# Cross attention with split operands: both tail products of neighbouring PV steps ahead of their small products

## The reference, cut to what matters

```python
q = split_heads(x @ w_q)                       # 20 heads of 32
k, v = split_heads(text @ w_k), split_heads(text @ w_v)
out_text = softmax(q k^T / sqrt(32)) v
k_ip, v_ip = split_heads(ip @ w_k_ip), split_heads(ip @ w_v_ip)
out_ip = softmax(q k_ip^T / sqrt(32) + mask_ip) v_ip   # mask from the boxes and the query's place
out = merge_heads(out_text + out_ip) @ w_out + b_out + x
```

## Time and profile before

| | us |
|---|---|
| median of 3 runs | 709.34 |
| lowest and highest | 707.80, 711.19 |
| the profiled execution | 710.03 |
| its span, first to last instruction | 708.0 |
| TensorE busy with matmuls in the span | 685.1 (97%) |
| TensorE's weight loads | 633.3 (89%) |
| VectorE busy | 534.3 (75%) |
| ScalarE busy | 291.0 (41%) |
| GpSimd busy | 215.0 (30%) |
| mean granted TensorE clock, share of full | 0.988 |

### The profile page before, as it was taken

The page is one execution under the profiler, slowest core; times in us unless marked ns, Lnnn a source line. Parts: engine busy times, 40 slices in busy tenths (PEclk is TensorE's granted clock), DMA queues, the critical chain, the costliest instruction groups (busy, mean ns, idle before and its releaser), DMA issues.

```text
span 708.0 us, 19244 instructions
## 1 busy us (share of the span) xinstructions
PE 685.1 (97%) x6570; PEld 633.3 (89%) x6570; DVE 534.3 (75%) x1689; ACT 291.0 (41%) x636; POOL 215.0 (30%) x371
## 2 busy tenths in 40 slices
PE   6998999999999999999999999999999999999987
PEld 4787678989899999999998999999999999899876
DVE  3344468797879788887978787878888797978773
ACT  1132353351617262534435161726353442516160
POOL 5312006042423324150504242332415050424233
PEclk9999999999999999999999999999999999999989
DMA  9979616444436262534444353626353444434320
GB/s 297 379 212 213 152 37 142 130 105 111 123 83 163 67 173 77 147 84 140 100 133 103 105 130 77 171 67 168 82 142 90 134 101 121 112 82 118 80 64 37
DMA packets 52512, 89.40 MB, mean 126 GB/s; under 512 B 9440, under 2 KB 23520, under 8 KB 52460
## 3 DMA queue, kind: packets, MB, share of 16 engines
q1 hardware_dynamic: 51024, 86.09, 45.3%
q10 hardware_dynamic: 1068, 1.66, 0.9%
q0 software_dynamic: 384, 1.18, 0.8%
HBM read 39.21 MB, written 10.62 MB: 70 GB/s over the span
## 4 chain that ended last, share of the span: by engine, by line
PE 84%; SPq 5%; DMA 4%; DVE 3%; issue 1%; ACTq 1%; ACT 1%; POOL 0%; DVEq 0%
PE psum L1086 38%; PE psum L1147 9%; PE psum L1193 9%; PE psum L1172 5%; PE psum L1177 5%; SPq L414 4%; PE psum L1016 3%; PE psum L1201 3%; PE psum L1202 2%; PE psum L1216 2%; PE psum L954 2%; PE psum L1046 1%; PE psum L1199 1%; DMA q_stack<-mask_scratch 1%; DMA k_stack<-k_lo 1%
## 5 line engine op out<-in xcount | busy, mean ns | idle before, releaser
L570 POOL TENSOR_TENSOR attn<-o_parts 128x128 f32<-128x128 f32 x160 | 73.0, 457 | 418.3 <-DVE o_parts L901 388.0
L860 DVE TENSOR_REDUCE neg_max<-psum 128x2 f32<-128x292 f32 x320 | 144.6, 452 | 48.8 <-PE psum L1147 48.5
L1086 PE MATMUL psum<-wo_both,at_hi 128*128 128x320 f32 x640 | 153.6, 314 | 0.0
L1147 PE MATMUL psum<-k_stack,q_stack 104*128 104x154 f32 x640 | 113.6, 288 | 5.5 <-DMA q_stack<-mask_scratch 3.5
L1086 PE MATMUL psum<-xt_hi,wq_hi 128*128 128x256 f32 x400 | 114.6, 287 | 1.1 <-DVE q_lo L852 1.1
L1086 PE MATMUL psum<-xt_lo,wq_hi 128*128 128x256 f32 x400 | 111.7, 279 | 0.0
L1086 PE MATMUL psum<-xt_hi,wq_lo 128*128 128x256 f32 x400 | 111.5, 279 | 0.0
L1086 PEld LDWEIGHTS psum<-wo_both,at_hi 128*128 128x128 f32 x640 | 110.1, 189 | 0.0
L888 DVE TENSOR_TENSOR p_lo<-psum,p_hi 128x512 f16<-128x512 f32 x160 | 107.8, 682 | 2.8 <-ACT psum L714 2.7
L712 ACT ACTIVATE p_hi<-psum 128x512 f16<-128x512 f32 x160 | 95.2, 595 | 29.7 <-PE psum L1172 29.5
L1193 PE MATMUL psum<-v_tail,p_tail 128*128 128x264 f32 x320 | 102.4, 401 | 1.8 <-ACT p_tail L716 0.9
(11 more groups left out here) (96 smaller groups left out, 1268.3 us busy)
## 6 DMA issues: line engine op xcount, KB each, us to landing
q_stack<-q_hi SPq DMA_DIRECT2D x128, 96.0 KB
x_in<-in_x SPq DMA_DIRECT2D x16, 640.0 KB, 5.3
x_res<-in_x SPq DMA_DIRECT2D x16, 640.0 KB, 5.5
out<-out_sb SPq DMA_DIRECT2D x32, 320.0 KB
q_stack<-q_hi SPq DMA_DIRECT2D x128, 64.0 KB
q_stack<-q_lo SPq DMA_DIRECT2D x60, 96.0 KB
q_stack<-q_lo SPq DMA_DIRECT2D x60, 64.0 KB
q_stack<-aux_a SPq DMA_DIRECT2D x48, 64.0 KB, 2.4
```

The source lines that it names most:

```text
L570: nc.gpsimd.tensor_tensor(cols, o_parts[:, qt, 0:4, :], o_parts[:, qt, 4:8, :], ALU.add).then_inc(att_half, 1)
L860: nc.vector.tensor_reduce(dst[:, :, 0], src[:, :, 0:TEXT], AX_X, ALU.max, negate=True)
L1086: last = nc.tensor.matmul(ps, l(c), r(c), start=(i == 0), stop=(i == len(terms) - 1))
L1147: last = nc.tensor.matmul(scores[sc % 2][:, i * CTX:(i + 1) * CTX], q_stack[0:ROW_MAX, query_slot(h), P * qt:P * (qt + 1)], k_stack[batch] ...
```

## The change

The constant `TAILS_AHEAD = 2` is new. At a PV step TensorE looks at up to two PV steps in a row from there on. It issues the waits and the tail product of each that has not had its tail yet, and only then the 12 small products of its own step. A step whose tail has been issued already goes straight to its small products. In the run of three this gives tail (1,1), tail (2,0), small (1,1), small (2,0), tail (2,1), small (2,1). In the run of two it gives tail (3,0), tail (3,1), small (3,0), small (3,1). Nothing is added or taken away, and only TensorE's stream is altered.

```diff
+TAILS_AHEAD = 2
...
+            def neighbours(order, at):
+
+                run = []
+                while len(run) < TAILS_AHEAD and at < len(order) and order[at][1] == "PV":
+                    run.append(tuple(order[at][2]))
+                    at += 1
+                return run
...
-                for stage, kind, args, gen, sc in it.steps():
+                order, tails = it.steps(), []
+                for at, (stage, kind, args, gen, sc) in enumerate(order):
...
                     if kind == "PV":
+                        run = neighbours(order, at)
+                        for g, qt in run if at not in tails else ():
+                            if isinstance(t, int) and t == 1 and (g, qt) == (0, 0):
+
+                                pe.wait_ge(s_vc, 5)
+                                pe.wait_ge(s_vsplit, 3 * V_PARTS)
+                            if qt == 0:
+
+                                pe.wait_ge(exp_done, t * ST_ALL - ST_ALL + 1 + max(ST_TURN[(g, u)] for u in range(3)))
+                                pe.wait_ge(p_split, t * 10 - 10 + 2 * g + 2)
+                            ahead = run.index((g, qt))
+                            free_general(it, gen + ahead)
+
+                            nc.tensor.matmul(product_1[it.general_bank(gen + ahead)][:, 0:8, :],
+                                             p_tail[:, -g % P_SLOTS, P * qt:P * (qt + 1)],
+                                             v_tail[batch][:, g, :].rearrange("p (e d) -> p e d", d=VW), start=True, stop=False)
+                            tails.append(at + ahead)
                         g, qt = args
-                        if isinstance(t, int) and t == 1 and (g, qt) == (0, 0):
-
-                            pe.wait_ge(s_vc, 5)
-                            pe.wait_ge(s_vsplit, 3 * V_PARTS)
-                        if qt == 0:
-
-                            pe.wait_ge(exp_done, t * ST_ALL - ST_ALL + 1 + max(ST_TURN[(g, u)] for u in range(3)))
-                            pe.wait_ge(p_split, t * 10 - 10 + 2 * g + 2)
-                        free_general(it, gen)
                         queries = slice(P * qt, P * (qt + 1))
-
-                        nc.tensor.matmul(product_1[it.general_bank(gen)][:, 0:8, :], p_tail[:, -g % P_SLOTS, queries],
-                                         v_tail[batch][:, g, :].rearrange("p (e d) -> p e d", d=VW), start=True, stop=False)
                         for j in range(4):
```

## The result

The changed kernel has a median of 711.55 us in 20 runs, the kernel before 708.81 us in 20. The ratio is 1.0041 with a 95% interval of 1.0024 to 1.0058: 0.4% slower, small but clear of no change. The profiled execution has a span of 710.3 us against 708.0.

A forecast was written before the change was run, and what follows sets the result against it. PE was taken to bound nearly each step; 12 blocks at 0.22 us, three at 0 and 0.2 in the last add 2.8 us to the median of 709.34, giving 712.1 us, range 708.3 to 714.6.

The forecast's parts named there:

- What the change gains: On PE, tails (2,0) and (3,1) behind another tail each save 0.08 us of weight load: 0.16 us a block.
- Rival 2: A tail behind a tail hides no weight load; PE loses 0.08 us more a block, 713.3 us; chance 0.08.
- What it delays: Small products of (1,1) end 0.45 us later, DVE's chain slips, tail (3,1) waits for PV(2,0)'s bank: 0.22 us a block.
- Tail (3,0) reacts 0.07 us after p_lo: PE's load for tail (3,0) starts 0.07 us after DVE ends p_lo of ST(3,1), at 264.48 against 264.47 today.
- Made good in blocks 1, 8 and 15: PE's waits there for query DMAs, 0.48, 0.26 and 0.26 us, cover the 0.22 us delay, so these blocks cost nothing.
- The last block: Tail (4,0) follows p_lo of ST(4,1), which has DVE's delay of 0.20 us: a cost of 0.2 us.
- The sum: Whole kernel: 12 blocks at 0.22 us, 3 at 0, the last 0.2: together 2.8 us, 712.1 us, 0.4% slower.
- Rivals 1 and 3: 1: DVE's slip stays covered, block 38.24 us, 706.8 us, chance 0.14; 3: slip reaches PE whole, 716.1 us, chance 0.06.
- rival 3: DVE still late at PE's score banks, up to 0.45 us a block, block over 38.75 us, 716.1 us; chance 0.06.

The follow-up runs named there:

- pairs_same_group: Changed kernel, but tails paired as (2,0) with (2,1) and (3,0) with (3,1); against the kernel before: ratio 0.9958, in a second comparison 0.9984.
- late_readout: Kernel before, TensorE order untouched; DVE waits for PV(2,0) too before reading out PV(1,1): 714.8 us, ratio 1.0107 to the kernel before.
- three_ahead: Changed kernel, but in the run of three all three tails come before any small products: 718.41 us, ratio 1.0141 to the kernel before.
- low_part_first: Changed kernel, with DVE writing p_lo of ST(3,1) before the readout of PV(1,1): 711.98 us, ratio 1.0050 to the kernel before.
- pair_first: Changed kernel, but only tail (2,0) drawn ahead, behind tail (1,1); (3,0) and (3,1) as before: 709.3 us, ratio 0.9995 to the kernel before.

## Why the prediction was right, point by point

- *What the change gains.* Right. A tail behind a tail starts after 0.22 us, tail (2,1) came 0.08 us sooner. Rival 2 does not hold for these loads. What reaches the end of a block was a little less, on the mean 0.11 and 0.13 us for two pairs in place of 0.16; in pairs_same_group about 0.02 us of it is lost again between the start of ST(4,2) and tail (4,0) (2.33 us in place of 2.30), and in its first profile the second loop gained only 0.08 us. Why is open.
- *What it delays.* Right, to 0.01 us: reciprocal at 1.44 us (1.44 forecast), readout of (2,0) at 3.67, load of tail (3,1) at 3.72, ST(4,2) at 4.96 (4.95), block 38.62 (38.62). That this chain is the cause is shown from four sides: without the slip there is no cost (pairs_same_group), with a slip and no new order there is one (late_readout, where a larger slip comes in at tail (3,0)), a larger slip costs more (three_ahead), a shortened chain on DVE costs less (low_part_first).
- *Tail (3,0) reacts 0.07 us after p_lo.* A size that was off. That figure came from the first block, which is written out singly. In the loops it is 0.12 us (pair_first, late_readout, and the change itself: `p_lo` ends at 265.60, the load starts at 265.73). In the full change it did not move the time, since tail (3,1) waits longer anyway.
- *Made good in blocks 1, 8 and 15.* Wrong for blocks 8 and 15. The DMA waits there did not cover the delay: behind them PE waits for DVE, and DVE was as late as PE. The delay passed through block 8 as through its neighbours (to the next tail (1,1) it grew from 1.80 to 2.03 us, 378.52 - 376.72 and 417.27 - 415.23), and through block 15 at least as far as tail (4,1), 0.22 us. Two blocks at 0.22 us, 0.4 us of the sum, were left out wrongly. For block 1 it is open. Its DMA wait did not shrink (0.48 us before, 0.54 after), and from its tail (1,1) to the next one it took 40.83 us in place of 39.95; but this stretch scatters from 39.95 to 42.51 us over the nine profiles.
- *The last block.* Right: tail (4,0) comes 0.17 us later after tail (1,1) (6.50 in place of 6.33), 0.2 was forecast.
- *The sum.* It came out at 2.8 us forecast and 2.7 us measured (711.55 - 708.81), but partly by chance: with blocks 8 and 15 it would have been 3.3 us (14 x 0.22 + 0.2), and the interval of 1.7 to 4.1 us does not tell the two apart. In the two profiles, the delay is 0.48 us at block 2, grows by 3.01 us to block 15 and ends at 2.3 us. Part of the last stretch ran faster in the profile after, at a granted clock of 0.95 of full speed in place of 0.84 (part of the stretch at the lower level of 1.2 GHz). From the windows of both, before and after:

```profile
670.00:702.00 32.00, 28.12 (x246) 24.50 (x247) 20.80 (x63) 14.16 (x29) 11.98 (x21) 0.84 0.16 43
...
670.00:702.00 32.00, 26.26 (x251) 22.92 (x251) 22.62 (x72) 14.08 (x29) 11.46 (x21) 0.95 0.15 42
```

- *Rivals 1 and 3.* Neither. No block of the change is near 38.24. In the first loop none is above 38.75; in the second, where a block took 38.47 to 38.52 us before, they take 38.70 to 38.77. The longest is past the forecast's mark by 0.02 us, but the price there is 0.22 to 0.30 us and not the 0.45 of rival 3. DVE had again 0.70 us of idle time ahead of Q 4 (0.67 before), so its backlog ended there.

## What to carry to other kernels

A tuned order holds back work for a reason that the busy engine's own profile does not show: each product drawn forward delays the signal of those behind it. Before moving one, look for who starts within 0.05 us of that signal, follow its list in order, and ask which later wait its last item feeds. Here the remedy was to choose the pair whose signal has slack: before the change DVE came to PV(2,0) 0.55 us after its last small product had ended, to PV(1,1) only 0.04 us. The remedy is worth 0.1 us of a block. And a wait in the profile is cover only if nothing else would have been waited for in its place; compare with a block that lacks it.

## What the runs showed of the hardware that was not expected

- PE reacts to DVE at different speeds: 0.05 us at tail (3,1), which waits for one thing, 0.07 us for tail (3,0) in an iteration written out singly, 0.12 us for the same tail in a loop iteration. Both of the last are found in one profile: after the change it is 0.07 us in blocks 1, 8, 15 and 16 and 0.12 to 0.13 us in the loops. In a loop, further waits and their register arithmetic stand between; that it is the register arithmetic was not tried by itself.
- Runs of the kernel before lie between 702.5 and 711.2 us beside the change, and between 702.5 and 715.8 us in all three comparisons, 1.9% apart. Its single blocks repeat to 0.02 us in the first loop; in all profiles and loops the blocks of one loop lie within 0.13 us. The scatter of the profiles sits in the first 146 us (tail (1,1) of block 2 at 143.42 to 148.20 in the nine profiles) and from about 670 us on, where the granted clock changes. A question of 0.1 us a block is answered by 13 like blocks in one profile, and hardly by whole runs.
